# Two shared single PSUM banks, and the output projections of two head quads summed before one add

## What is computed

```python
x = x + 0.5 * _L0_ffn_ref(_layernorm(x), ...)   # 8 experts, top 2, capacity, gelu gate
x = x + _L0_attn_ref(_layernorm(x), ...)        # 16 heads of 8, causal, linear bias
x = x + 0.5 * _L0_ffn_ref(_layernorm(x), ...)
x = x + 0.5 * _L1_ffn_ref(_layernorm(x), ...)   # latent attention, 16 heads, + 8 small experts, top 2
x = x + _L1_attn_ref(_layernorm(x), ...)        # conv, state scan, gated, then a gelu ffn
x = x + 0.5 * _L1_ffn_ref(_layernorm(x), ...)
```

## Time and profile before

| | |
|---|---|
| median of 3 runs | 1571.46 us |
| the profiled execution, its time | 1566.18 us |
| its span, first to last instruction | 1564.1 us |
| TensorE busy | 1377.9 us, 88% |
| VectorE busy | 1025.2 us, 66% |
| ScalarE busy | 883.0 us, 56% |
| GpSimd busy | 403.4 us, 26% |
| mean granted TensorE clock | 0.944 |
| chain that ended last, TensorE's share | 67% |

### The profile page before, as it was taken

The page is one execution under the profiler, slowest core; times in us unless marked ns, Lnnn a source line. Parts: engine busy times, 40 slices in busy tenths (PEclk is TensorE's granted clock), DMA queues, the critical chain, the costliest instruction groups (busy, mean ns, idle before and its releaser), DMA issues.

```text
span 1564.1 us, 27086 instructions
## 1 busy us (share of the span) xinstructions
PE 1377.9 (88%) x10934; PEld 571.9 (37%) x10934; DVE 1025.2 (66%) x1541; ACT 883.0 (56%) x1110; POOL 403.4 (26%) x331
## 2 busy tenths in 40 slices
PE   4999967788885999989899988999988998789997
PEld 3544433233322444433333323333432433333342
DVE  3433358788844546697868757688768756776735
ACT  2322335577783346266566586856668785336672
POOL 5465400011101656452220223012304014202000
PEclk8899978899997999999999999999998999889998
DMA  5512001100001632011111000110110102001100
GB/s 158 110 54 54 6 14 44 25 2 1 2 2 19 152 68 54 6 29 22 32 22 21 1 17 6 22 31 2 22 21 1 22 5 48 8 8 22 22 1 14
DMA packets 30279, 45.80 MB, mean 29 GB/s; under 512 B 5886, under 2 KB 10686, under 8 KB 30110
## 3 DMA queue, kind: packets, MB, share of 16 engines
q1 hardware_dynamic: 30156, 44.08, 12.9%
HBM read 25.39 MB, written 1.18 MB: 17 GB/s over the span
## 4 chain that ended last, share of the span: by engine, by line
PE 67%; ACT 10%; DVE 8%; issue 8%; SPq 4%; POOL 2%; DMA 1%; POOLq 0%; DVEq 0%; ACTq 0%
PE ps L1283 13%; PE ps L1330 10%; ACT PR L1361 5%; PE ps L1269 4%; PE ps L1078 3%; PE ps L1633 3%; PE ps L1660 3%; SPq L1547 3%; PE ps L1634 3%; PE ps L1635 3%; PE ps L1341 3%; PE ps L1748 3%; PE ps L1261 2%; PE ps L1092 2%; DVE BM L1393 2%
## 5 line engine op out<-in xcount | busy, mean ns | idle before, releaser
L1361 ACT ACTIVATE PR<-ps 128x1024 f32<-128x1024 f32 x432 | 433.6, 1023 | 275.6 <-PE ps L1290 151.3
L1393 DVE TENSOR_REDUCE BM<-ps 128x2 f32<-128x1024 f32 (+2 forms) x384 | 348.4, 950 | 50.1 <-PE ps L1269 48.9
L1283 PE MATMUL ps<-QS,KS 48*128 48x512 f16 (+7 forms) x2688 | 308.0, 331 | 53.8 <-ACT PR L1361 38.7
L1330 PE MATMUL ps<-PR,VS 128*32 128x512 f32 (+3 forms) x2304 | 238.7, 505 | 4.0 <-ACT PR L1361 2.4
L1283 PEld LDWEIGHTS ps<-QS,KS 48*128 48x128 f16 (+1 forms) x2688 | 107.3, 95 | 234.7 <-ACT PR L1361 111.2
L1269 PE MATMUL ps<-KS,QS 48*128 48x128 f16 (+2 forms) x1728 | 166.9, 282 | 24.6 <-DVE BM L1393 21.1
L1427 POOL TENSOR_TENSOR ON<-OS,RX 128x512 f32<-128x512 f32 x48 | 62.1, 1296 | 477.3 <-ACT RX L1375 473.6
L1386 DVE TENSOR_REDUCE BM<-ps 128x8 f32<-128x1024 f32 x96 | 116.8, 1219 | 45.5 <-PE ps L1269 45.2
L1269 PEld LDWEIGHTS ps<-KS,QS 48*128 48x128 f16 x1728 | 71.2, 97 | 154.2 <-DVE BM L1393 70.2
L1070 POOL TENSOR_TENSOR HL<-HL,PR 128x512 f32<-128x512 f32 x64 | 83.0, 1298 | 83.3 <-ACT HL L1116 80.3
L1146 DVE SCALAR_TENSOR_TENSOR HL<-ps,HL 128x512 f32<-128x512 f32 x64 | 44.2, 691 | 86.4 <-POOL HL L1070 86.4
(11 more groups left out here) (303 smaller groups left out, 2173.4 us busy)
## 6 DMA issues: line engine op xcount, KB each, us to landing
PR<-gates SPq DMA_DIRECT2D x32, 512.0 KB, 13.6
QS<-KS SPq DMA_DIRECT2D x64, 128.0 KB
QS<-KS SPq DMA_DIRECT2D x64, 64.0 KB
WM<-W_in SPq DMA_DIRECT2D x1, 2048.0 KB, 9.3
QS<-HL SPq DMA_DIRECT2D x48, 32.0 KB
KS<-HL SPq DMA_DIRECT2D x48, 32.0 KB
QS<-CT SPq DMA_DIRECT2D x96, 2.0 KB
KS<-KS SPq DMA_DIRECT2D x8, 128.0 KB, 2.4
```

What stands on the lines that cost most here:

```text
L1283: ins = pe.matmul(ps[pair][:, w, off:off + cols], KS[rows, ks, kt * P:(kt + 1) * P], QS[rows, qs, (ph + 1) * TT - cols:(ph + 1) * TT], sta ...
L1330: ins = pe.matmul(OUT[32 * j:32 * j + 32, TT - cols:TT], v, PR[:, buf, j, off:off + cols], start=(g == 0), stop=(g == NGRP[ph] - 1))
L1361: act.activation(dst, src, ACT.Exp, scale=0.125 if lat else 1.0).then_inc(sig["exp"], 1)
L1393: ins = dve.tensor_reduce(BM[:, ph, p, :, qt - 4 * ph, part], bnk[:, :, off:off + nk * P], AX.X, ALU.max)
```

## The change

1. OUT and MISC are no more. The pool "misc" has two banks, and the planner gives every single-bank task, the `pv` sum of a phase and the `ed` sums among them, whichever of the two is free. A phase's `pv` sum holds its bank from its first product to `ev`. The first `pv` of a phase no longer waits for the `ev` of the phase before, but for the previous owner of its own bank.
2. `proj` is done for odd quads only. It is then two products into one bank, that of the even quad before it (from ON) and its own (from OS), and one `add` follows. The planner's cost of `proj` is 1.9 instead of 1.0.
3. For odd quads `on` writes the normalised output over OS instead of into ON. So `ev` of an even quad waits for `proj` of the odd quad before it (of an odd quad, still for `on` of the quad before), and `on` waits for `proj` in even quads only.

```diff
-    ROOM = {"pair": 3, "misc": 1, "nr": 2}
+    ROOM = {"pair": 3, "misc": 2, "nr": 2}
...
                 if g == 0:
-                    need += [self.phase_before(n, ph, "ev"), *values]
+                    need += values
                 add("PE", "pv", ("pv", n, ph, g), *need)
...
-            add("ACT", "ev", ("ev", n, ph), last, ("on", n - 1, ph) if n else None)
+            self.take(("pv", n, ph, 0), "misc", add("ACT", "ev", ("ev", n, ph), last, ("on" if n % 2 else "proj", n - 1, ph) if n else None))
...
-            add("POOL", "on", ("on", n, ph), ("rx", n, ph), ("proj", n - 1, ph) if n else None)
+            add("POOL", "on", ("on", n, ph), ("rx", n, ph), ("proj", n - 1, ph) if n and n % 2 == 0 else None)
+            if n % 2 == 0:
+                continue
...
+        def single(plan, task):
+            return ps[3][:, plan.slot[task], :]
...
-                pe.matmul(MISC, w_o[:, n % NQ, :], ON[:, hq(ph)], start=True, stop=True).then_inc(sig["proj"], 1)
+                pe.matmul(single(plan, task), w_o[:, n % NQ - 1, :], ON[:, hq(ph)], start=True, stop=False)
+                pe.matmul(single(plan, task), w_o[:, n % NQ, :], OS[:, hq(ph)], start=False, stop=True).then_inc(sig["proj"], 1)
...
-            pool.tensor_tensor(ON[:, hq(ph)], OS[:, hq(ph)], RX[:, hq(ph)], ALU.mult).then_inc(sig["on"], 1)
+            pool.tensor_tensor((ON, OS)[n % 2][:, hq(ph)], OS[:, hq(ph)], RX[:, hq(ph)], ALU.mult).then_inc(sig["on"], 1)
```

More of the change, by code:

```diff
@@ L1672, in pe_late @@
                     src = YA if kn == 6 else XT
-                    pe.matmul(MISC, mean_w[:, :], src[:, tsl(t)], start=True, stop=True).then_inc(sig["mean"], 1)
+                    pe.matmul(one, mean_w[:, :], src[:, tsl(t)], start=True, stop=True).then_inc(sig["mean"], 1)
                 elif kind == "var":
@@ L1676, in pe_late @@
                     pe.wait_ge(sig["sq"], c("sq", kn, t))
-                    pe.matmul(MISC, mean_w[:, :], nr1(plan, kn, t), start=True, stop=True).then_inc(sig["var"], 1)
+                    pe.matmul(one, mean_w[:, :], nr1(plan, kn, t), start=True, stop=True).then_inc(sig["var"], 1)
                 elif kind == "key":
@@ L1681, in pe_late @@
                     pe.wait_ge(sig["scl"], c("scl", 4 * kk - 1, 2 * b + h))
-                    pe.matmul(MISC[0:64, :], w_kva[:, :], XN[:, tsl(2 * b + h)], start=True,
+                    pe.matmul(one[0:64, :], w_kva[:, :], XN[:, tsl(2 * b + h)], start=True,
                               stop=True).then_inc(sig["key"], 1)
@@ L1720, in pe_late @@
                     for i in range(4):
-                        ins = pe.matmul(MISC[0:24, i * P:(i + 1) * P], RTB[:, i, :], onesb[:, :], start=True, stop=True)
+                        ins = pe.matmul(one[0:24, i * P:(i + 1) * P], RTB[:, i, :], onesb[:, :], start=True, stop=True)
                     ins.then_inc(sig["gtr"], 1)
@@ L1747, in pe_late @@
                         n = rows_of(g)
-                        ins = pe.matmul(MISC, w_down1[0:n, g, :], ring_hf(r, t, g)[0:n, :], start=(g == 4), stop=(g == 3))
+                        ins = pe.matmul(one, w_down1[0:n, g, :], ring_hf(r, t, g)[0:n, :], start=(g == 4), stop=(g == 3))
                     ins.then_inc(sig["dn"], 1)
@@ L1752, in pe_late @@
                     pe.wait_ge(sig["scb"], c("scb", 5, t))
-                    pe.matmul(MISC, w_inp[:, ch, :], XN[:, tsl(t)], start=True, stop=True).then_inc(sig["inp"], 1)
+                    pe.matmul(one, w_inp[:, ch, :], XN[:, tsl(t)], start=True, stop=True).then_inc(sig["inp"], 1)
                 elif kind == "dbc":
@@ L1756, in pe_late @@
                     pe.wait_ge(sig["cv"], c("cv", t // 2, 2))
-                    pe.matmul(MISC, w_dbc[:, w, :], half(A1, t), start=True, stop=True).then_inc(sig["dbc"], 1)
+                    pe.matmul(one, w_dbc[:, w, :], half(A1, t), start=True, stop=True).then_inc(sig["dbc"], 1)
                 elif kind == "outp":
@@ L1760, in pe_late @@
                     pe.wait_ge(sig["st3"], c("st3", t // 2))
-                    pe.matmul(MISC, w_outp[:, :], half(A3, t), start=True, stop=True).then_inc(sig["outp"], 1)
+                    pe.matmul(one, w_outp[:, :], half(A3, t), start=True, stop=True).then_inc(sig["outp"], 1)
                 elif kind == "f1":
@@ L1764, in pe_late @@
                     pe.wait_ge(sig["scb"], c("scb", 6, t))
-                    pe.matmul(MISC, w_f1[:, ch, :], XN[:, tsl(t)], start=True, stop=True).then_inc(sig["f1"], 1)
+                    pe.matmul(one, w_f1[:, ch, :], XN[:, tsl(t)], start=True, stop=True).then_inc(sig["f1"], 1)
                 elif kind == "f2":
@@ L1769, in pe_late @@
                     for ch in range(2):
-                        ins = pe.matmul(MISC, w_f2[:, ch, :], f1_room(t)[:, ch * TT:(ch + 1) * TT], start=(ch == 0),
+                        ins = pe.matmul(one, w_f2[:, ch, :], f1_room(t)[:, ch * TT:(ch + 1) * TT], start=(ch == 0),
                                         stop=(ch == 1))
```

91 lines of the change are left out of this document (47 added, 44 removed).

## The result

The change takes 1518.45 us (median of 4 runs, 1509.58 to 1519.35) against 1572.36 for the kernel before (4 runs, 1568.02 to 1574.67). The ratio is 0.9648, 95% interval 0.9606 to 0.969: 3.5% faster, some 54 us. The forecast was 1551 us with a range from 1533, so the direction was right and the size was not: the gain is more than twice the forecast.

What follows compares the result with a forecast made beforehand. TensorE, busy 1377.9 of 1564.1 us, was taken as the bound. Terms -22.7 + 6.4 - 3.2 - 1.3 = -20.8 us took the median from 1571.46 to 1550.7, forecast as 1551 us, range 1533 to 1570.

Steps and rivals of the forecast that it cites:

- Nothing is removed there. The gain can only be idle time and clock.: TensorE's work: the same 48 projection products, masks, scores and sums before and after, so no gain from removed work.
- The hole before quad 12 closes: 1310 to 1400 us becomes as dense as 1400 to 1500: 13.5 us idle time and 9.2 us clock, 22.7 us saved.
- the late start: Quad 12's first unit starts only after quads 0 to 11 use up all 216 score steps; ending this saves 22.7 us.
- The new dense place at quad 8: Between quads 7 and 8, both batch-1 expert tiles lie together: 1.9 us idle time and 4.5 us clock, cost 6.4 us.
- Rivals B and D: Batch-1 experts starve TensorE at quad 8: hole moves (B, 1567.6 us, chance 0.10) or doubles (D, 1590 us, chance 0.06).
- The old dense place in quad 4 thins: In quad 4, the second `dn` of batch 0 moves 12 score steps back: 3.2 us saved.
- 24 additions fewer: On VectorE, 16.4 us less busy time, mostly covered by TensorE; 8% of it counted, 1.3 us saved.
- No wait of `pv` for `ev`: Between phases, the 585 ns copy is already hidden by score steps and units: gain 0; 27.5 us were all exposed.
- The first attention: First attention, a quad repeating every 28.42 us: its lists hardly move, so 0, between -3 and +3 us.
- The end: From the last score steps on, TensorE's order is the same and only banks differ: 0.
- Rival A: Between 650 and 1300 us, the second bank thins idle time everywhere: another 14.2 us saved, 1536.5 us, chance 0.15.

Runs made afterwards that it cites:

- ninth experiment: The change with one more VectorE reduction before each of its 24 additions, about 16 us of VectorE work: 1525.31 us, ratio 0.971 to the kernel before.
- e12: The change with the planner's cost of an addition 0.75 instead of 0.68: 1530.28 us, ratio 0.9742 to the kernel before.
- e3: The change with quad 12's builds made to wait in the planner, so its units start only after all 216 score steps: 1526.48 us, ratio 0.9724 to before.
- e8: The kernel before with the planner's cost of a transpose 0.25 instead of 0.2: 1554.83 us, ratio 0.9866 to the unaltered kernel before.

## Why the prediction was wrong, point by point

**"Nothing is removed there. The gain can only be idle time and clock."** Right: TensorE's 10934 instructions are the same, 27.7 us of the gain are idle time and 19.3 busy time, most of that by a better clock.

**"The hole before quad 12 closes" (-22.7 us).** It did close, and the stretch behaves as it was priced: 1310 to 1400 us, taken against the plain stretch as in the forecast, has 5.1 - 6.1 = -1.0 us of excess idle time and 84.88 x 0.02 = 1.7 us of clock loss, so 22.0 of the 22.7 us are gone from it. But the price of a stretch is not the price of its cause. Putting the late start back brought back 15.4 us of excess in the stretch, clock loss included, and cost the program 8 us by the medians, 10 in the profiled executions. Why the two differ was not followed.

**"The new dense place at quad 8" (+6.4 us).** Right in place and size: 1050 to 1125 us has 7.6 - 5.1 = 2.6 us of excess idle time and 67.36 x 0.07 = 4.7 us of clock loss, 7.3 us. Rivals B and D, in which this place becomes as bad as the old one or worse, did not happen.

**"The old dense place in quad 4 thins" (-3.2 us).** Too small by this pricing. Between 850 and 950 us excess idle time and clock loss were 7.4 + 8.6 = 16.0 us before and 1.3 + 2.8 = 4.1 in the change: 11.9 us less. Taken from 800 us on, so that the down products which the change has at 846 us are inside in both, it is 5.7 + 9.4 = 15.1 and 2.7 + 4.1 = 6.8, 8.3 us less. The forecast read only half of that stretch and credited half of that.

**"24 additions fewer" (-1.3 us).** Perhaps too small: the ninth experiment points to some 7 us for the same work, but its interval does not exclude the forecast. VectorE's 8% share of the chain as the rate at which its work costs time was neither shown nor refuted.

**"No wait of `pv` for `ev`", gain 0.** It holds for the wait itself: after the change, too, no row of TensorE's matrix products names the copy of OS, and the copy's waiters are VectorE and five weight loads, 4.5 us in all:

```profile
  DVE RX L1422: 58.2, 17
  PEld ps L1348: 3.0, 1
  PEld ps L1337: 1.5, 4
```

The page "Perfetto Trace Analysis" of the Trainium skill (section on matmuls) says that independent groups should rotate through banks so that evacuation overlaps. The traces show little to win by that here: no matrix product waited for the copy before. Had all copies been exposed, the forecast's rows gave 27.5 us. With the fence back in list and program the change still keeps 2.5% of its 3.5%. Since that run has another list as well, what the overlap alone is worth stays open, but it is not the bulk.

**"The first attention", 0 within 3.** It ends 3.0 us earlier (474.41 against 477.40 us), at the bound. **"The end", 0:** from the last copy on, 37.2 us instead of 39.4: 1.3 us less idle time, and 0.9 less busy time at a clock of 0.90 instead of 0.86.

**The step that failed** is the frame of the sum: it took the list of before as a fair one, and looked for the few places at which the change repaired it. The runs showed that the list was the slowest of the four lists of its own planner that were timed (ratios 1, 0.9928, 0.9866, 0.9732), and that of the change the fastest of its four (0.9648, 0.9726, 0.9742, 0.9784). The edit of the planner's cost from 1.0 to 1.9, which the prediction did not price at all, alone took 2.7% off the kernel before. Banks and pairs at equal numbers are worth 24 us on average; the other 30 us of the 54 are then the list's. That the 24 us lie close to the 20.8 of the sum is chance, since the sum priced places in the order and not banks and pairs. Its largest term was mis-sized too: the late start, put at 22.7 us, cost 8 to 10 when it was put back, in a milder form. Nothing in the one profile of before showed this; only other lists of the same program did. Nor can a forecast of this kernel be held to 0.3%: thirteen executions of before in one comparison took from 1564.11 to 1584.24 us.

Rival A (idle time thinned everywhere, 1536 us, 0.15) came nearest, and in part for its reason: much of the gain lies outside the hole. But the runs do not show that waits for MISC were behind it: the list of before on two banks was slower, not faster.

**What stays open.** What makes one list better than another, apart from the hole: no experiment moved another single place. How much of a difference in clock is the list's and how much the execution's: the change and e12 differ by 7.7 us of idle time and 5.7 of busy time, and two executions of the same order differed by 4.7 us of busy time in 535. And how the gain divides between banks and pairs.

## What to carry to other kernels

Where a planner or scheduler writes the order, a change of resources or costs also draws a new order, and a new order of the same instructions was worth up to 2.7% here. So time one or two copies of the old kernel with a meaningless change of the planner's numbers before a result of one or two per cent is put down to the change, and compare old and new at the same numbers. To price a hole, put it back alone: the excess of its stretch (15 us) was more than what its cause cost (8 to 10 us). Set profiled executions against each other over the same work, and look first at how far they differ where their lists are the same. And a second buffer shared between roles pays only with an order made for it; with the old order its new waits made the kernel 1% slower.

## What was not expected of the hardware

The clock moves the time by as many us as idle time does here, and it moves without any change of the program. The thirteen executions of before named above had mean granted clocks from 0.946 in the fastest to 0.934 in the slowest. The order moves it too: the four executions of e3 had 0.947 to 0.958, the five of e8 0.937 to 0.945. The profiled ones are the extremes of the two: the same 10934 TensorE instructions were busy 1350.6 us in e3 (0.958) and 1387.4 us in e8 (0.937), 37 us apart at nearly the same idle time (170.3 and 173.2 us), so part of the 37 us is the execution's. About half of it lies in one place: from 840 to 1100 us e8's mean granted clock is 0.91 at only 19.9 us of idle time in 260, against 0.99 in e3:

```profile
840.00:1100.00 260.00, 240.11 (x1908) 93.25 (x1905) 182.30 (x295) 182.08 (x220) 49.05 (x31) 0.91 0.09 18
```

The page "TensorE: Matmul & The Clock Gate" of the Trainium skill (Part 1) says that the gate follows how busy TensorE has recently been. If so, idle time costs by how it is bunched and not by its sum. These two runs agree with that as far as the sum goes; how it was bunched was not examined.
